# Issuing half of a matrix's loads from GpSimd's DMA queue instead of SyncE's

## The reference, cut to what matters

```python
def reference(x, adj, weight, W, b):          # x 8192x64, adj 8192x8192, all float32
    h = relu(layernorm(x))
    t = [h, adj @ h]
    for _ in range(2, 4):
        t.append(2.0 * (adj @ t[-1]) - t[-2])
    x = x + einsum('kni,kio->no', stack(t), weight)
    h = relu(layernorm(x))
    deg = clip(sum(adj, axis=1) + 1, 1)
    z = concat([h, (adj @ h + h) / deg]) @ W + b
    out = relu(z)
    return x + out / max(norm(out), 1e-12)
```

## Time and profile before

| | |
|---|---|
| median of 3 runs | 2939.23 us |
| runs | 2846.58, 2939.23, 2948.15 us |
| span of the profiled execution | 2906.5 us |
| mean granted TensorE clock (share of full) | 0.883 |
| busy: TensorE, VectorE, ScalarE, GpSimd | 77%, 56%, 25%, 1% |
| moved by DMA | 689.56 MB, mean 237 GB/s |

### The profile page before, as it was taken

One profiled execution on the slowest core, in us unless ns is written; L12 is line 12 of the kernel. 1 busy time (PEld: TensorE's weight loads), 2 busy tenths in 40 slices (PEclk: granted clock), 3 DMA queues, 4 the chain that ended last, 5 costly groups with the idle time before them and its releaser, 6 DMA issues.

```text
span 2906.5 us, 20534 instructions
## 1 busy us (share of the span) xinstructions
PE 2229.9 (77%) x6792; PEld 946.0 (33%) x6792; DVE 1637.0 (56%) x1204; ACT 729.8 (25%) x2243; POOL 35.8 (1%) x73
## 2 busy tenths in 40 slices
PE   2566877798888889979888878778776786777666
PEld 0122333343343334434333333333232232322222
DVE  5555665556545556555455566555545455577666
ACT  4556656666555553000000000000000000000000
POOL 0000000000000000000000000000000000001001
PEclk9788889888999999999999999889888888889877
DMA  9999999999999999999999999999999999999996
GB/s 220 238 239 259 275 266 265 252 266 277 229 228 234 232 231 219 230 228 235 235 235 232 233 220 231 233 223 226 223 222 223 227 229 236 246 309 283 231 229 142
DMA packets 428333, 689.56 MB, mean 237 GB/s; under 512 B 56514, under 2 KB 130242, under 8 KB 428226
## 3 DMA queue, kind: packets, MB, share of 16 engines
q1 hardware_dynamic: 425344, 685.95, 105.2%
q0 software_dynamic: 2048, 2.10, 0.3%
q10 hardware_dynamic: 834, 0.20, 0.0%
HBM read 685.97 MB, written 2.10 MB: 237 GB/s over the span
## 4 chain that ended last, share of the span: by engine, by line
SPq 71%; DMA 10%; PE 9%; issue 4%; ACT 3%; DVE 2%; POOL 0%; DVEq 0%
SPq L315 71%; DMA ring<-in_adj_dram 10%; PE ps_pair L721 6%; ACT ring L370 3%; PE ps_single L727 2%; DVE ring L577 2%; SPq L304 0%; PE ps_lin L666 0%; PE ps_lin L669 0%; PE ps_lin L681 0%; PE ps_tr L685 0%; DVE vec L573 0%; PE ps_lin L682 0%; POOL out_dram L330 0%; PE ps_lin L672 0%
## 5 line engine op out<-in xcount | busy, mean ns | idle before, releaser
L577 DVE STREAM_TRANSPOSE ring<-ring 128x2048 f32<-128x2048 f32 x640 | 1431.6, 2283 | 1073.6 <-DMA ring<-in_adj_dram 713.3
L721 PE MATMUL ps_pair<-ring,vec 128*128 128x512 f32 x2880 | 1356.9, 629 | 263.0 <-DVE ring L577 246.4
L721 PEld LDWEIGHTS ps_pair<-ring,vec 128*128 128x128 f32 x2880 | 570.1, 202 | 1017.1 <-issue 869.2
L727 PE MATMUL ps_single<-ring,vec 128*64 128x512 f32 x2240 | 623.1, 697 | 329.5 <-DVE ring L577 326.2
L370 ACT ACTIVATE ring<-ring 128x512 f32<-128x512 f32 x1024 | 627.9, 614 | 416.0 <-DMA ring<-in_adj_dram 416.0
L727 PEld LDWEIGHTS ps_single<-ring,vec 128*64 128x64 f32 x2240 | 168.0, 156 | 707.8 <-issue 474.6
L397 ACT ACTIVATE sum_s<-ps_single 128x512 f32<-128x512 f32 x64 | 37.7, 589 | 634.9 <-PE ps_pair L721 461.2
L370 ACT ACTIVATION_READ_ACCUMULATOR ring<-ring 128x1 f32 x1024 | 191.3, 187 | 0.0
L399 ACT ACTIVATE sum_p<-ps_pair 128x512 f32<-128x512 f32 x45 | 26.5, 590 | 499.5 <-PE ps_pair L721 499.5
L348 ACT ACTIVATE stat<-stat,eps 128x4 f32<-128x4 f32 (+1 forms) x20 | 6.0, 299 | 312.5 <-DVE stat L519 310.1
L573 DVE STREAM_TRANSPOSE vec<-ring 128x512 f32<-128x512 f32 x40 | 25.1, 682 | 91.5 <-issue 81.5
(11 more groups left out here) (94 smaller groups left out, 542.0 us busy)
## 6 DMA issues: line engine op xcount, KB each, us to landing
ring<-in_adj_dram SPq DMA_DIRECT2D x2320, 256.0 KB, 13.7
ring<-in_adj_dram SPq DMA_DIRECT2D x192, 192.0 KB, 12.8
ring<-in_adj_dram SPq DMA_DIRECT2D x192, 128.0 KB, 9.3
ring<-in_adj_dram SPq DMA_DIRECT2D x192, 64.0 KB, 6.0
res<-in_x_dram SPq DMA_DIRECT2D x8, 256.0 KB, 5.9
out_dram<-vec POOLq DMA_DIRECT2D x64, 32.0 KB, 7.1
tmp<-in_L_gnn_weight_dram ACTq DMA_DIRECT2D x2, 64.0 KB
row_sums<-in_L_gnn_W_dram ACTq DMA_DIRECT2D x2, 32.0 KB
```

The costliest lines, as they stand in the source:

```text
L577: nc.vector.transpose(blocks, blocks).then_inc(s_turned, 1)
L721: last = nc.tensor.matmul(ps_pair[n % 2][:], vec[:, CB * J + c, :, :], moving, start=(k == pair_at[0] and c == 0), stop=(k == pair_at[-1] ...
L727: last = nc.tensor.matmul(ps_single[n % 2][half:half + F, :], vec[:, CB * J + c, single_slot, :], moving, start=(k == single_at[0] and c < 2),
```

## The change

The loads of quadrants 0 and 1 (partitions 0 to 63) stay on SP's queue. Those of quadrants 2 and 3 (partitions 64 to 127) are issued by GpSimd. Each half of a strip has its own semaphores, and ScalarE and VectorE wait for both. GpSimd waits for room in the ring as SP does. The output stores stand among its loads: before GpSimd waits for room, it stores those finished rows whose epilogue begins more than STORE_LAG units before the unit that it would wait for; what is left is stored at the end.

```diff
+STORE_LAG = 6
...
-        s_strip = [sem(f"strip_loaded{i}") for i in range(NSEM)]
+        s_low = [sem(f"strip_low_loaded{i}") for i in range(NSEM)]
+        s_high = [sem(f"strip_high_loaded{i}") for i in range(NSEM)]
...
                 for ar in range(Q):
-                    for a in range(Q):
+                    for a in (0, 1):
...
-                        sp.dma_start(dst, src).then_inc(s_strip[i % NSEM], 16)
+                        sp.dma_start(dst, src).then_inc(s_low[i % NSEM], 16)
...
-            for n, C in sorted((n, C) for (sweep, C), n in row_index.items() if sweep == 4):
+            def store_row(n, C):
+
                 pool.wait_ge(s_row, n + 1)
                 for a in range(Q):
                     pool.dma_start(out_v[a, :, CB * C:CB * C + CB, :],
                                    vec[32 * a:32 * a + 32, CB * C:CB * C + CB, 0, :]).then_inc(s_out, 16)
+
+            finished = sorted((n, C) for (sweep, C), n in row_index.items() if sweep == 4)
+            stored = 0
+            for i, (n, J0, w, _) in enumerate(strips):
+                row = rows[n]
+                if places[i][1] > 0:
+                    free_at = strip_start[places[i][1]]
+                    while stored < len(finished) and begin_at[finished[stored][0]] + STORE_LAG < free_at:
+                        store_row(*finished[stored])
+                        stored += 1
+                    pool.wait_ge(s_unit, free_at)
+                for ar in range(Q):
+                    for a in (2, 3):
+                        col = a * QN + J0 * UC
+                        src = adj_v[ar, :, CB * row.C:CB * row.C + CB, col:col + w * UC]
+                        dst = strip_of(i)[32 * a:32 * a + 32, ar:G:Q, :]
+                        pool.dma_start(dst, src).then_inc(s_high[i % NSEM], 16)
+            for n, C in finished[stored:]:
+                store_row(n, C)
             pool.wait_ge(s_out, 16 * Q * NB)
...
-                act.wait_ge(s_strip[i % NSEM], 16 * Q * Q * (i // NSEM + 1))
+                act.wait_ge(s_low[i % NSEM], 8 * Q * Q * (i // NSEM + 1))
+                act.wait_ge(s_high[i % NSEM], 8 * Q * Q * (i // NSEM + 1))
...
-                dve.wait_ge(s_strip[i % NSEM], 16 * Q * Q * (i // NSEM + 1))
+                dve.wait_ge(s_low[i % NSEM], 8 * Q * Q * (i // NSEM + 1))
+                dve.wait_ge(s_high[i % NSEM], 8 * Q * Q * (i // NSEM + 1))
```

## The result

The changed kernel takes 2661.03 us (median of 4 runs, 2646.59 to 2672.75); the kernel before, run beside it, 2929.42 us. The ratio is 0.928, 95% interval [0.915, 0.942]. The quotient of the medians is 0.908; the ratio stands above it because it leaves out executions of the kernel before that were over 1.5% above its fastest. The forecast was 2445 us with a range from 2330 to 2930: the direction was right and the time lies inside the range, but it is 216 us over the forecast. The gain is 7% by the ratio and 9% by the medians, where 17% was forecast.

What follows compares the result with a forecast made beforehand. DMA engines, at a rate set by something packets share, were taken as the bound. At 311 GB/s, 43 + 885 + 505 + 680 + 300 = 2413 us of span, plus 32.7, gave 2446, taken as 2445 us (-17%); range 2330 to 2930.

Steps and rivals of the forecast that it cites:

- What bounds it: Adj loads: full DMA engines at 228 to 248 GB/s by stage, limited by something packets share; SP's issuing no bound.
- Steps 1, 2, 5, 6: Half the loads leave SP, worth nothing; GpSimd issues them, 0.55 us each; both issuers wait for ring room; second strip wait, 0.
- rival D: GpSimd's issue of loads becomes the bound from 2.0 us per load; 3330 us at 2.3 us; chance 0.11.
- Step 3: Adj loads: two queues' packets alternate between partition halves, raising the rate to 311 GB/s; the whole gain.
- The bounds of the term, 228 and 325: Loading rate in GB/s: 228 is no gain (stage three), 325 the best stretch of the trace.
- The sign that was set for being right: First stage: over 290 GB/s at a DMA share near or under 1.
- rival B: Adj loads: one queue empties before the other or turns are long; 262 GB/s, 2692 us; chance 0.14.
- A's own range: Whole kernel, the forecast case that packets alternate: 2380 to 2570 us; chance 0.58.
- Step 4: Stage times from 311 GB/s or engine floors: start 43, then 885, 505, 680, 300; span 2413 us.
- The other floors: Engine time when no data is missing: 849 us in sweep 1, 662 in stage three, VectorE's 243 in stage four.
- The 32.7 us around the span: Whole kernel: median 2939.2 over profiled span 2906.5, carried over to the new span, giving 2446 us.

Runs made afterwards that it cites:

- e2: Kernel before, one SP queue, loops swapped so all four row groups of one quadrant are loaded before the next quadrant: 3316.14 us.
- e1: Kernel before, one SP queue, quadrants issued in the order 0, 2, 1, 3 instead of 0, 1, 2, 3: 2687.72 us.
- e8: Changed kernel with half of each load left out once the ring has been filled, all waits and compute kept, output not the reference's: 2207.31 us.
- e14: e10 with ScalarE issuing before a row's evacuation only loads whose room comes free at least four units before the row's end, others behind it: 2528.27 us.
- e9: Changed kernel with GpSimd waiting until x has landed before it issues its first load: 2647.14 us.
- e5: Changed kernel with the upper half issued from ScalarE's queue from sweep 2 on, GpSimd keeping it in sweep 1: 2636.25 us.
- e12: Changed kernel with strips of up to two blocks instead of four, SP's packets 1 KB and GpSimd's still 4 KB: 2977.88 us.
- e10: e5 with x first at the start and ScalarE issuing loads that have room before it waits for a variance: 2624.75 us.

## Why the prediction was right in direction and wrong in size

**What bounds it** (the 16 engines at a rate that is set by something their packets share, and not SP's issuing): right. That it goes by halves is shown by e2 and e1. An estimate from the Trainium skill's port figure (SBUF — State Buffer, "Door 1: the DMA port swizzle") was 218 GB/s for one half of the partitions; e2 measures 201 to 215. The rule that spoke against the change, in the Trainium skill (DMA: Bandwidth & Descriptors, "Rules for kernel authors"), that transfers to disjoint halves serialize, does not hold here: 354 GB/s with both halves against 208 with one.

**Steps 1, 2, 5, 6.** GpSimd's issue: 551 ns each for 1448 loads, against the 0.55 us taken; 256 B and 2 KB runs cost the same, rival D is out; and its premise that 2 KB runs are not joined is wrong, as the packets of 4096 bytes show. (The first of the four stores took 0.68 us, so they didn't all keep their length, as the step has it; nothing hangs on it.) SP's issue stayed off the path. Both queues wait for room as foreseen, the stores cost 26 us of waiting on an engine that is mostly idle. What the second wait per strip costs was not measured by itself; VectorE's busy time is the same, 1637.1 against 1637.0 us.

**Step 3 is the one that failed**, as put: "I take 311, near the upper end, because the alternation is there all the time and not by luck". Two things were wrong in it. The engines do not alternate evenly in bytes: the page of before shows one queue at work, and I took the second to be served alike, though its packets are twice as large. And the alternation isn't there all the time: 2 to 1 shares finish one half first, and the rest is loaded at the rate of one half, 208; this is 24% of the time (above). Where 311 GB/s was taken, the stages run at 268, 254, 265 and 234. The sign that was set for being right, over 290 in the first stage, did not come. I had this mechanism as rival B ("one queue empties before the other"), at 262 GB/s and 2692 us with a chance of 0.14. The measured 254 to 268 GB/s and 2661 us are B; A's own range, 2380 to 2570 us, was missed. The bounds of the term, 228 and 325, were rates of one queue; the upper one was no bound, since equal queues reach 354.

**Step 4**, stage by stage against the forecast: start 43 -> 75, sweep 2 505 -> 507, and in the three stages that the rate sets 885 -> 979, 680 -> 763, 300 -> 347. That is 32 + 2 + 94 + 83 + 47 = 258 us. That sweep 2 came out to 2 us is luck. The step had TensorE as its bound, at 481 us and some bubbles, with the loads done in 410. Measured, the loads take 127 MB at 254 GB/s = 502 us at a share of 1.02, TensorE can do the sweep in 449 (e8, e14), the chain of waits through it lies for 48% on TensorE's main product and for 42% on the loads and SP's issuing of them, and TensorE's idle time before the main product has not nearly gone but fallen from 68.2 to 38.9 us:

```profile
L745 PE MATMUL ps_pair<-ring,vec 128*128 128x512 f32 x965 | 432.0, 607 | 38.9 <-DVE ring L601 37.4 <-DVE vec L530 1.4
```

A rate too high and a floor too high gave the right sum. The other floors were too high in sweeps 1 and 3 and 20 us too low in the last stage (e8). The 32 us at the start were missed altogether: I costed the moved loads by their place among the adj loads and not by the x loads that they had stood behind in SP's queue. e9 puts their worth at about 14 us, which is hardly more than the spread of the runs.

**The 32.7 us around the span** were mis-sized: after, the profiled execution took 2672.75 us at a span of 2670.9, so the true surplus is 2 us, and what I carried over was the spread between executions of the kernel before. Here the profiled span lies 10 us over the median. 2446 + 258 - 33 - 10 = 2661.

## What to carry to other kernels

When all DMA engines are busy and the rate still changes from stretch to stretch at the same kind of transfer, ask which partitions the packets in flight write at one time, and try to give each half of the partitions to a queue of its own; if only one queue is to be had, shorten the runs on one half. Before splitting work between two queues, compare their packet sizes: the queue with the larger packets takes the larger share of the engines, and the other half of the data is then late. And an operation that is moved to another queue also leaves behind what it was queued after: look at what it now overtakes, and on an engine with work of its own, at what it now delays.

## What the runs showed of the hardware that was not expected

- Loads to partitions 0 to 63 alone stay at 208 GB/s with all 16 engines full; both halves from two equal queues reach 354 GB/s (1200 to 1210 us of e5). The halves here are also halves of adj's columns.
- Two queues are served about packet for packet: 840 and 953 packets with parts of adj in 18 us, and 141 and 137 in 3 us of e12; by bytes 2.1 to 1 at 4 KB against 2 KB, 4.1 to 1 at 4 KB against 1 KB.
- One queue that changes halves has a wide spread: e1's runs spread over 8% and those of the kernel before beside it over 6% (2848.21 to 3012.97 us), while the changed kernel's spread over 1%, e10's over 0.2% and e2's, with its long runs, over 0.5%. Two mixed queues spread over 1 to 2%. Why is not shown.
- Two queues that each write both halves are no faster than one (2844 to 2985 us). This was found three times and not explained.
